# Where four half batches of head data are read back: all inside the two token stages, none in attention

## The reference

```python
x = x + _L0_xattn_ref(ctx_1024, ctx_1024, _layernorm(x), mask, ...)   # 16 heads, keys and values from ctx
x = x + _L0_ffn_ref(_layernorm(x), ...)      # causal attention over 16 heads, then the experts
x = x + _L1_xattn_ref(_layernorm(x), ctx_1024, ...)
x = x + _L1_ffn_ref(_layernorm(x), ...)
```

## Time and profile before

| | |
|---|---|
| median of the runs | 2046.16 us (2043.82 to 2049.41) |
| the profiled execution, its own time | 2052.6 us |
| its span | 2050.4 us |
| granted TensorE clock, mean share of full speed | 0.923 |
| TensorE (PE) busy | 1755.2 us, 86% |
| VectorE (DVE) busy | 1326.9 us, 65% |
| ScalarE (ACT) busy | 1103.9 us, 54% |
| GpSimd (POOL) busy | 569.3 us, 28% |
| mean DMA rate | 84 GB/s |

### The profile page before, as it was taken

One profiled execution on the slowest core, in us unless ns is written; L12 is line 12 of the kernel. 1 busy time (PEld: TensorE's weight loads), 2 busy tenths in 40 slices (PEclk: granted clock), 3 DMA queues, 4 the chain that ended last, 5 costly groups with the idle time before them and its releaser, 6 DMA issues. The chain is left out here.

```text
span 2050.4 us, 40249 instructions
## 1 busy us (share of the span) xinstructions
PE 1755.2 (86%) x13889; PEld 1073.1 (52%) x13890; DVE 1326.9 (65%) x2362; ACT 1103.9 (54%) x2105; POOL 569.3 (28%) x479
## 2 busy tenths in 40 slices
PE   7568878889797899997795799999998469999987
PEld 4322222222574444443674688888887245665555
DVE  6478988898465777774576354555554457777753
ACT  6338777788453677776541344444443246555551
POOL 5233988550330222222277000000000422222000
PEclk9779999999998899999765899999999689999999
DMA  5533565430243122110533111111111511111000
GB/s 187 146 110 113 194 199 180 135 120 4 85 129 103 32 71 62 47 43 25 234 111 114 60 47 46 46 46 46 46 47 42 177 42 52 52 52 51 21 11 21
DMA packets 104067, 171.70 MB, mean 84 GB/s; under 512 B 16104, under 2 KB 78464, under 8 KB 100096
## 3 DMA queue, kind: packets, MB, share of 16 engines
q1 hardware_dynamic: 97216, 152.14, 23.3%
q0 software_dynamic: 6144, 16.79, 2.5%
q10 hardware_dynamic: 576, 1.05, 0.1%
HBM read 103.34 MB, written 61.87 MB: 81 GB/s over the span
## 5 line engine op out<-in xcount | busy, mean ns | idle before, releaser
L1101 DVE TENSOR_REDUCE a_nm<-a_psS 128x2 f32<-128x1024 f32 (+1 forms) x384 | 442.6, 1176 | 54.6 <-PE a_psS L951 35.6
L1081 ACT ACTIVATE a_prob<-a_psE 128x512 f32<-128x512 f32 (+2 forms) x660 | 335.2, 561 | 98.0 <-PE a_psE L973 96.7
L973 PE MATMUL a_psE<-wall 51*128 51x512 f16 (+3 forms) x1024 | 291.7, 351 | 37.1 <-ACT a_prob L1081 12.8
L951 PE MATMUL a_psS<-wall 49*128 49x512 f16 (+4 forms) x1024 | 287.2, 363 | 26.0 <-PEq L2515 13.0
L1723 ACT ACTIVATE rows<-ex_psH,ex_b 128x256 f32<-128x256 f32 x312 | 130.5, 469 | 217.3 <-PE ex_psH L1754 217.3
L1754 PE MATMUL ex_psH<-ex_xT,wall 128*128 128x256 f16 x1872 | 232.7, 275 | 7.4 <-issue 4.0
L973 PEld LDWEIGHTS a_psE<-wall 51*128 51x128 f16 x1024 | 76.8, 94 | 296.3 <-ACT a_prob L1081 137.5
L1768 PE MATMUL ex_psY<-wall,ex_hl 128*128 x1872 | 229.9, 273 | 1.4 <-DVEq L1670 0.4
L1754 PEld LDWEIGHTS ex_psH<-ex_xT,wall 128*128 x1872 | 182.7, 98 | 34.6 <-issue 12.7
L1768 PEld LDWEIGHTS ex_psY<-wall,ex_hl 128*128 128x128 f16 x1872 | 179.1, 98 | 32.3 <-issue 11.0
L1681 DVE CAST ex_hl<-rows 128x512 f16<-128x512 f32 x156 | 66.6, 427 | 182.8 <-ACT rows L1723 181.1
(11 more groups left out here) (282 smaller groups left out, 3127.6 us busy)
## 6 DMA issues: line engine op xcount, KB each, us to landing
s_qk<-wall SPq DMA_DIRECT2D x32, 512.0 KB, 3.2
wall<-s_qk SPq DMA_DIRECT2D x128, 128.0 KB
xall<-in_w SPq DMA_DIRECT2D x16, 1024.0 KB, 11.5
s_ew<-xall SPq DMA_DIRECT2D x16, 1024.0 KB, 9.3
wall<-s_ew SPq DMA_DIRECT2D x14, 1024.0 KB, 10.4
rows<-s_xs SPq DMA_DIRECT2D x39, 256.0 KB, 2.7
s_ys<-ex_yo SPq DMA_DIRECT2D x39, 256.0 KB, 2.2
t_xin<-in_x SPq DMA_DIRECT2D x16, 512.0 KB, 5.0
```

What stands on the lines that cost most here:

```text
L951: last = pe.matmul(psS[:, bank, col:col + n], Q6[s][at:at + SROWS, pr, t * P:(t + 1) * P], K6[s][at:at + SROWS, pr, 0:n], start=True, stop ...
L973: last = pe.matmul(psE[unit % NE][:, col:col + w], K6[s][at:at + EROWS, pr, t * P:(t + 1) * P], Q6[s][at:at + EROWS, pr, S - w:S], start=T ...
L1081: act.activation(prob_of(unit)[:, 0:w], psE[unit % NE][:, 0:w], ACT.Exp, scale=ESC).then_inc(p_ready, 1)
L1101: dve.tensor_reduce(nm[G % NM_BUF][:, t, :, i], psS[:, at:at + 2, 0:n], axis=AX.X, op=ALU.max, negate=True).then_inc(s_free, 1)
```

## The change

The condition that spread one call over each iteration is replaced by a table. `FIRST_LOADS` becomes 4, so that the list `late` in attention is empty and attention fetches nothing at G = 0 and G = 1.

```diff
-FIRST_LOADS = 3
+FIRST_LOADS = 4
+EARLY_LOADS = {2: ((0, 0),), 3: ((0, 1),), 4: ((1, 0), (1, 1)), 5: ((2, 0),), 6: ((2, 1), (3, 0)), 7: ((3, 1),)}
...
-                if 2 <= n < 2 + 2 * FIRST_LOADS:
-                    hb = (n - 2) // 2
-                    sp.wait_ge(qk_out[0], 32)
+                for hb, e in EARLY_LOADS.get(n, ()):
+                    sp.wait_ge(qk_out[hb // 2], 32)
                     sp.wait_ge(m_out, 16)
                     sp.wait_ge(set_done, CONSTS + hb + 1)
-                    heads.load(sp, hb, n % 2, scr["qk"], scr["mask"])
+                    heads.load(sp, hb, e, scr["qk"], scr["mask"])
```

More of the change, by code:

```diff
@@ L495, in _ @@
                                  ).then_inc(qk_out[n % 2], 16)
-                if 2 <= n < 2 + 2 * FIRST_LOADS:
-                    hb = (n - 2) // 2
-                    sp.wait_ge(qk_out[0], 32)
+                for hb, e in EARLY_LOADS.get(n, ()):
+                    sp.wait_ge(qk_out[hb // 2], 32)
                     sp.wait_ge(q_set, hb + 1)
-                    heads.load(sp, hb, n % 2, scr["qk"], None)
+                    heads.load(sp, hb, e, scr["qk"], None)
             for p in range(2):
```

## The result

The changed kernel takes 2058.22 us (median of 20 runs) against 2046.45 us for the kernel before in 20 runs: the ratio is 1.0058, with a 95% interval of 1.0036 to 1.008. That is 11.9 us slower, between 7.4 and 16.4. The forecast was 13.4 us and 2059.6.

The account below looks back on a forecast made before the run. The prediction took the token stages to be bound by SyncE's order of loads and stores, with broadcast head loads draining on two DMA engines. 5.7 + 5.7 + 2.0 = 13.4 us on 2046.2 gave 2059.6 us, range 2052 to 2065.

Parts of the forecast that it names:

- The first double call: First token stage, n = 4: two head loads ahead of batch 7's token load delay VectorE's start on it, +5.7 us.
- The iteration n = 5: First token stage: one head load as before with no token load behind it, so no cost.
- The second double call: First token stage, n = 6: two head loads delay the last store, and attention waits for it, +5.7 us.
- The forecast of the landing: End of the first token stage: the last Q store would land in about 10.7 us instead of 5.0.
- SyncE's wait at L265: End of the first token stage: SyncE's wait for the last store would grow from 1.3 to about 7 us.
- The second token stage: Its n = 6: a second head load makes the last Q store land later, +2.0 us (0 to 4).
- the landing of its last store: End of the second token stage: the last Q store would land in 5.2 us, not 3.2.
- Attention: G = 0 and 1: taking the head loads out changes nothing (0 to -2.2 us).
- Rival D: Attention gains up to 2.2 us, more than the token stages lose, so not slower: 2044.0 us; chance 0.03.
- Rival A: Added loads spread over all engines; only SyncE's issue at n = 4 counts, +3.1 us: 2049.3 us; chance 0.05.
- rival B: The two engines catch up before the last store; only n = 4 costs: 2052.0 to 2053 us; chance 0.08.
- rival C: A second load costs as much as a first: 7.7 + 7.7 + 4 = 19.4 us, 2065.6 us; chance 0.09.

Follow-up runs that it names:

- e1: The change made only in the first token stage and its attention stage of the kernel before; 2053.99 us, ratio 1.0047.
- e3: Kernel before, first token stage only: both loads of half batch 1 together at n = 4, none at n = 5; 2049.36 us, ratio 1.0011.
- e2: The change made only in the second token stage and its attention stage of the kernel before; 2046.08 us, ratio 0.9999.
- e4: Kernel before, first token stage only: double call at n = 6, one more load at n = 7, the last in attention; 2053.89 us, ratio 1.0032.
- e11: Kernel before, with the repeated rows of the head loads as an inner dimension of the source, same transfer sizes; 2037.11 us, ratio 0.9937.
- e12: Changed kernel, with the repeated rows of the head loads as an inner dimension of the source, same transfer sizes; 2036.19 us, ratio 0.9947.
- e6: Changed kernel, with each 128 KB broadcast transfer split into two of 16 rows; 2036.92 us, ratio 0.9951 to the kernel before.
- e10: Changed kernel, with broadcast transfers split into 16-row ones and token loads issued ahead of head loads; 2033.25 us, ratio 0.9924 to the kernel before.
- e5: Kernel before, with each 128 KB broadcast transfer split into two of 16 rows; 2039.19 us, ratio 0.9949.
- e14: Changed kernel, with the repetition as an inner dimension and token loads issued ahead of head loads; 2028.68 us, ratio 0.9907 to the kernel before.
- e13: Kernel before, with the repetition as an inner dimension and token loads issued ahead of head loads; 2030.09 us, ratio 0.9907.

## Why the prediction was right, point by point

1. **The first double call** was forecast at +5.7 us. Against the profile before it measures +4.8 in the changed kernel, +5.4 in e1 and +5.2 in e3. But the 10.62 us of idle time in that profile is the longest of the three without a double call at n = 4 (e2 has 9.81, e4 9.48). The mean of the three with it, 15.8, less the mean of the three without, 10.0, is 5.8. The step was right, and so was its size.
2. **The iteration n = 5** was taken at nothing. In the changed kernel, the K and Q stores of batch 6 land in 6.1 and 5.6 us exactly as before, and e3, with no load there at all, has the same tail.
3. **The second double call**, +5.7, was measured at +5.8 in the changed kernel and in e1, and +6.0 in e4. The forecast of the landing, 10.7 us, came out to the digit. What was wrong is a detail of the evidence: I said SyncE's wait at L265 would be about 7 us, and it is 3.6. The reason stands in the last section.
4. **The second token stage**, +2.0, measured 1.8 at e2's barrier and 3.5 at the changed kernel's. The mechanism was right. The size was worked out from an execution in which TensorE was slow at the last K product, and holds for such a one; that the profile taken was of that kind was chance. At the full clock the term is 3.5, inside the range of 0 to 4 but nearly twice what I said. The 5.2 us that I gave for the landing of its last store was 4.9 in e2 and 6.7 in the changed kernel, for the same reason.
5. **Attention**, nothing: the step with the head load in it was 11.22 us before and 11.25 without in the changed kernel. In e2 and e3, with the same layout and load, it was 12.8, at a lower clock. So a small return from taking the load out, up to 1.6 us in some executions, isn't excluded. Rival D is out: it needed token stages that lose under 2.2 us.

By the marks the change costs 5.8 + 5.8 us and 1.8 to 3.5, together 13.4 to 15.1 us, beside 11.9 (7.4 to 16.4) in the timed ratio. The forecast of 13.4 lies in that interval; that it came so near is more than the timing can confirm. Rival A, issue alone, needed 3.1 us in all and is near what e11 and e12 look like; rival B fell with the tail of e4; rival C, 7.7 us for each of the first two, fell against 5.8, though its 4 for the second token stage was nearer than my 2.0. The Trainium skill's engine rate ("DMA: Bandwidth & Descriptors", "Specifications") would have given about 11 us, an estimate from the page's figure; the interval holds both. For one head load that rate makes 4.9 us, with the 0.35 of the small transfers, and the 49 GB/s of the trace 5.7; the tail of e4 grew by 6.0.

What stays open is the spread of the first attention stage, 396 to 416 us among executions, and the two lengths, some 6 us apart, of what follows the second token stage. The first is larger than anything that the change does, and no run here was made to explain either.

## What to carry to other kernels

Look at the DMA share while one kind of transfer drains alone: 0.12 means two engines of sixteen, and then that transfer is a queue of its own for every later one. A repetition belongs in an inner dimension of the access pattern, with rows outermost. Before moving prefetches, ask what is issued right behind them and who waits for it: here the place in the order was worth 0.7%; the layout with it brought the first score another 6.7 us forward, 0.2% in the times, whose intervals overlap; and the move itself cost 0.6%, or nothing that could be measured once both were mended. And a wait read in one profile is that of one execution: hold several of them against each other, at the same clock, before a microsecond of it is put into a sum.

## What the hardware showed beyond that

- The issue of a head load stalled SyncE. After the double call and two stores at the end of the first token stage, the four transfers of the last head load took 5.99 us to issue, of which the first alone 4.19 us, where it is 2.18 for all four in the kernel before. It is 6.21 in e1 and 5.95 in e4, and 2.13 in e3, 2.12 in e2 and 3.00 in e12. So it is seen in the three kernels with the double call at n = 6 on two engines, and to that size in none of the others (3.87 and 4.08 us for the six transfers of e6 and e10, beside 3.25 in e5). What in SyncE or in the queue it waits for, the trace doesn't show. That is why the wait at L265 was 3.6 us: SyncE arrived at it late. It cost nothing, as the store landed later still.
- How long TensorE stayed at the low clock after a wait did not follow the length of the wait. Its V product behind the wait for L350 took 2.79 us at the full clock of 2.4 GHz, after waits of 0.41, 1.04 and 1.68 us (e14, e13, e10). After waits of 2.43 to 11.65 us it came back at the low clock and took 4.35 to 5.30: 5.30 after 3.30 us in e5 and after 11.65 in e3, but 4.39 after 11.35 in e1.
